# Convolution, attention and expert network on one core: other engines and another order for the last layer norm

## What is computed

```python
logits = jnp.mean(x, axis=1) @ Wr + br                  # softmax twice, top 2 experts of 8
h = gelu(einsum('nd,edf->enf', xf, W1) + b1, approximate=False)
y = einsum('enf,efd->end', h, W2) + b2
out = einsum('ne,end->nd', w_dense, y).reshape(B, S, D)
out = _layer_norm(out + x, gamma, beta)                 # x: the normalised tokens
t = t + out                                             # then back to channels x positions
```

## Time and profile before

| | us |
|---|---|
| median of three runs | 403.71 |
| lowest, highest | 402.61, 403.78 |
| the profiled execution | 403.98 |
| its span (first to last instruction) | 402.2 |
| TensorE, VectorE, ScalarE, GpSimd busy | 385.0, 313.7, 276.1, 152.2 |

### The profile page before, as it was taken

How to read it: one execution, slowest core, us unless ns; L and a number is a source line. 1 busy time by engine, 2 the same in 40 slices (tenths; PEclk the granted TensorE clock), 3 DMA queues, 4 the chain that set the end, 5 groups by cost and what they waited for, 6 DMA issues and landing times.

```text
span 402.2 us, 5828 instructions
## 1 busy us (share of the span) xinstructions
PE 385.0 (96%) x1911; PEld 303.4 (75%) x1916; DVE 313.7 (78%) x699; ACT 276.1 (69%) x530; POOL 152.2 (38%) x205
## 2 busy tenths in 40 slices
PE   8899899999999999999998999999999999997994
PEld 3579896678788888888886888888877777645772
DVE  3798935779989988988998998999898174657745
ACT  1567665568788788888878888888877201557980
POOL 7200005485652754245325278668400000224015
PEclk9999998999999999999999999999999999999999
DMA  7990000000000000000000920000000000000002
GB/s 269 366 346 5 2 2 0 2 1 0 2 1 0 2 0 2 1 0 2 0 0 6 321 99 1 0 2 1 2 0 0 2 0 2 0 0 2 1 0 104
DMA packets 5263, 15.52 MB, mean 39 GB/s; under 512 B 690, under 2 KB 1906, under 8 KB 4978
## 3 DMA queue, kind: packets, MB, share of 16 engines
q1 hardware_dynamic: 4802, 14.19, 9.8%
q10 hardware_dynamic: 432, 0.97, 0.7%
HBM read 14.08 MB, written 1.08 MB: 38 GB/s over the span
## 4 chain that ended last, share of the span: by engine, by line
PE 81%; DVE 9%; ACT 4%; DMA 2%; issue 2%; POOLq 0%; POOL 0%; SPq 0%; ACTq 0%; DVEq 0%
PE ps L1167 13%; PE ps L1169 13%; PE ps L1168 13%; PE ps L1266 7%; DVE nmax_all L1634 3%; PE ps L1149 3%; PE ps L1151 3%; PE ps L1150 3%; PE ps L1050 3%; PE ps L1082 2%; PE ps L1089 2%; PE ps L907 2%; DMA xq<-laid_x_queries 2%; PE ps L1016 2%; PE ps L992 2%
## 5 line engine op out<-in xcount | busy, mean ns | idle before, releaser
L1634 DVE TENSOR_REDUCE nmax_all<-ps 128x1 f32<-128x1024 f32 x128 | 156.2, 1221 | 18.8 <-PE ps L1169 18.1
L780 ACT ACTIVATE exps<-ps,nmax_all 128x1024 bf16<-128x1024 f32 x128 | 142.6, 1114 | 35.1 <-DVE diag_all L1639 34.0
L1167 PE MATMUL ps<-qT_hi,kT_hi 128*128 128x512 f32 x256 | 103.0, 402 | 0.4 <-ACT exps L780 0.4
L1169 PE MATMUL ps<-qT_hi,kT_lo 128*128 128x512 f32 x256 | 100.8, 394 | 0.0
L1168 PE MATMUL ps<-qT_lo,kT_hi 128*128 128x512 f32 x256 | 100.4, 392 | 0.0
L1169 PEld LDWEIGHTS ps<-qT_hi,kT_lo 128*128 128x128 f32 x256 | 48.0, 188 | 10.9
L1167 PEld LDWEIGHTS ps<-qT_hi,kT_hi 128*128 128x128 f32 x256 | 48.1, 188 | 10.6 <-ACT exps L780 3.0
L1168 PEld LDWEIGHTS ps<-qT_lo,kT_hi 128*128 128x128 f32 x256 | 48.1, 188 | 7.4 <-issue 0.2
L525 POOL CAST qT_hi<-xq 128x341 fp32r<-128x341 f32 (+1 forms) x45 | 21.1, 468 | 85.6 <-ACT xq L762 84.3
L527 POOL TENSOR_TENSOR qT_lo<-xq,qT_hi 128x341 fp32r<-128x341 f32 (+1 forms) x45 | 41.6, 925 | 3.6
L1639 DVE CUSTOM_DVE_ANT_0 diag_junk<-ps,ident 128x128 f32<-128x128 f32 x128 | 35.8, 280 | 0.0
(11 more groups left out here) (230 smaller groups left out, 662.1 us busy)
## 6 DMA issues: line engine op xcount, KB each, us to landing
xs_first<-a_store SPq DMA_DIRECT2D x4, 512.0 KB, 5.7
xs_second<-a_store SPq DMA_DIRECT2D x4, 512.0 KB, 9.3
wqkv<-laid_qkv_weights SPq DMA_DIRECT2D x1, 1536.0 KB, 6.7
wvT<-laid_qkv_weights_T SPq DMA_DIRECT2D x1, 1536.0 KB, 10.0
xq<-laid_x_queries SPq DMA_DIRECT2D x2, 512.0 KB, 6.4
xk<-laid_x_keys SPq DMA_DIRECT2D x2, 512.0 KB, 7.9
x<-in_x SPq DMA_DIRECT2D x1, 1024.0 KB, 12.9
w<-in_L_ffn_W SPq DMA_DIRECT2D x1, 1024.0 KB
```

The source lines that it names most:

```text
L780: a.activation(exps[:, n % 2, :], slot(score_slot(col)), ACT.Exp, bias=nmax_all[:, col:col + 1], accum_out=sum_all[:, col:col + 1]).then_i ...
L1167: mm(tgt, keys_hi, qT_hi[:, u % 2, at], start=True, stop=False)
L1169: last = mm(tgt, keys_lo, qT_hi[:, u % 2, at], start=False, stop=True)
L1634: v.tensor_reduce(nmax_all[:, col:col + 1], slot(place), AX_X, ALU.max, negate=True)\
```

## The change

The changed kernel does the same arithmetic. It differs in the last 30 us:

- The rounding of gelu(7), the last step (`LAST_HIDDEN`): ScalarE leaves it out. VectorE rounds half 0 and GpSimd half 1, each with a semaphore of its own, `h_last`, in the place of `h_sb`.
- ScalarE takes the squares of chunks 0 and 1 after gelu(3) and gelu(5), not after gelu(4) and gelu(6), and loads the root's table right behind gelu(7); the square of chunk 2 comes after the root of part 0.
- TensorE takes the variances of chunk 1 one place earlier, and the spread of chunk 0 between the variances of chunks 2 and 3. Two groups of filler, seven matmuls, go.
- VectorE normalises chunk 0 before the reciprocal of chunk 3, and also adds `x1` for chunk 2; GpSimd adds it for chunks 0 and 1 only.

```diff
--- before.py
+++ after.py
@@ -293,12 +293,14 @@
         mb_ready, lg_ps, r_in, r_exp = (sem(n) for n in ("mb_ready", "logits_ps", "r_in", "r_exp"))
         idx_ready, w1_ready, w2_ready = sem("idx_ready"), sem("w1_ready"), sem("w2_ready")
         h_ps, h_full, h_sb, h_lo, y_ps = (sem(n) for n in ("h_ps", "h_full", "h_sb", "h_lo", "y_ps"))
+        h_last = [sem(f"h_last{f}") for f in range(2)]
         b2_centred, w2_mean_ready, w2_centred = (sem(n) for n in (
             "b2_centred", "w2_mean_ready", "w2_centred"))
         xn_hi_ready, xn_lo_ready = sem("xn_hi_ready"), sem("xn_lo_ready")
         late_square = sem("late_square")
         last_diagonal = sem("last_diagonal")
         out_ready = [sem(f"out_ready{c}") for c in range(4)]
+        LAST_HIDDEN = 7
 
 
         LN_PARTS = [((0, 1), (2, 3)), ((0, 1), (2, 3)), ((0, 1), (2,), (3,))]
@@ -602,11 +604,16 @@
                     g.tensor_tensor(w1_lo[:, b, k, :], chosen, w1_hi[:, b, k, :].bitcast(F32), ALU.subtract)\
                         .then_inc(w1_ready, 1)
 
+            n, f = LAST_HIDDEN, 1
+            pool.wait_ge(h_full, 2 * n + f + 1)
+            pool.wait_ge(y_ps, n - 1)
+            g.tensor_copy(hid_hi[:, n % 2, f, :], hid[:, n % 2, f, :]).then_inc(h_last[f], 1)
+
             for c in range(3):
                 pool.wait_ge(LN[2]["rstd"], 1 if c < 2 else 2)
                 lay_diagonal(2, c)
 
-            for c in range(3):
+            for c in range(2):
                 pool.wait_ge(LN[2]["out"], c + 1)
                 at = slice(c * 512, (c + 1) * 512)
                 g.tensor_tensor(conv_o[:, at], centred[:, at], x1[:, at], ALU.add).then_inc(out_ready[c], 1)
@@ -879,6 +886,8 @@
                         act.wait_ge(h_lo, 2 * n - 3 + f)
                     a.activation(hid[:, n % 2, f, :], bank(2 * (n % 2) + f), ACT.Gelu,
                                  bias=b1s[:, b, k, f:f + 1]).then_inc(h_full, 1)
+                    if n == LAST_HIDDEN:
+                        continue
                     act.wait_ge(h_full, 2 * n + f + 1)
                     if n >= 2:
 
@@ -887,11 +896,11 @@
 
             for n in range(8):
                 gelu(n)
-                if n in (4, 6):
-                    square(2, n // 2 - 2)
-            square(2, 2)
+                if n in (3, 5):
+                    square(2, n // 2 - 1)
             load_table(ACT.Sqrt)
             root(2, 0, 6)
+            square(2, 2)
             square(2, 3)
             root(2, 1, 7)
             root(2, 2, 0)
@@ -1353,7 +1362,10 @@
                 if k == 0 and c >= 2:
                     pe.wait_ge(LN[2]["centred"], c - 1)
                 for f in range(FC):
-                    pe.wait_ge(h_sb, 2 * n + f + 1)
+                    if n < LAST_HIDDEN:
+                        pe.wait_ge(h_sb, 2 * n + f + 1)
+                    else:
+                        pe.wait_ge(h_last[f], 1)
                     pe.wait_ge(h_lo, 2 * n + f + 1)
                     tgt = bank(4 + c % 2)
                     mm(tgt, w2_hi[:, b, k, f, :], hid_hi[:, n % 2, f, :], start=(k == 0 and f == 0), stop=False)
@@ -1370,13 +1382,13 @@
                 outputs(n)
                 if n + 2 < 8:
                     hidden(n + 2)
-                if n in (4, 6):
-                    variances(2, 0, 6, n // 2 - 2)
+                if n in (4, 5):
+                    variances(2, 0, 6, n - 4)
             variances(2, 1, 7, 2)
-            keep_warm(3, 4)
+            pe.wait_ge(LN[2]["diagonal"], 1)
+            spread(2, 0, 1)
             variances(2, 2, 0, 3)
-            keep_warm(3, 3)
-            for c in range(3):
+            for c in (1, 2):
                 pe.wait_ge(LN[2]["diagonal"], c + 1)
                 spread(2, c, 1 + c)
             pe.wait_ge(last_diagonal, 1)
@@ -1817,7 +1829,14 @@
             def hidden_remainder(n):
 
                 for f in range(FC):
-                    dve.wait_ge(h_sb, 2 * n + f + 1)
+                    if n < LAST_HIDDEN:
+                        dve.wait_ge(h_sb, 2 * n + f + 1)
+                    else:
+                        if f == 0:
+                            dve.wait_ge(h_full, 2 * n + 1)
+                            dve.wait_ge(y_ps, n - 1)
+                            v.tensor_copy(hid_hi[:, n % 2, f, :], hid[:, n % 2, f, :]).then_inc(h_last[f], 1)
+                        dve.wait_ge(h_last[f], 1)
                     if n >= 2:
 
                         dve.wait_ge(y_ps, n - 1)
@@ -1842,15 +1861,15 @@
                 if c < 3:
                     hidden_remainder(2 * c + 3)
             reciprocals(2, 1)
+            normalise_last(0, 1)
             reciprocals(2, 2)
             lay_diagonal(2, 3, last_diagonal)
-            normalise_last(0, 1)
-            normalise_last(1, 2)
-            normalise_last(2, 3)
-            normalise_last(3, 4)
-            dve.wait_ge(LN[2]["out"], 4)
-            at = slice(3 * 512, 4 * 512)
-            v.tensor_tensor(conv_o[:, at], centred[:, at], x1[:, at], ALU.add).then_inc(out_ready[3], 1)
+            for c in range(1, 4):
+                normalise_last(c, 1 + c)
+            for c in (2, 3):
+                dve.wait_ge(LN[2]["out"], c + 1)
+                at = slice(c * 512, (c + 1) * 512)
+                v.tensor_tensor(conv_o[:, at], centred[:, at], x1[:, at], ALU.add).then_inc(out_ready[c], 1)
 
 
 _INS = ["x", "L0_conv_wq", "L0_conv_bq", "L0_conv_wk", "L0_conv_bk", "L0_conv_wv", "L0_conv_bv",
```

## The result

The changed kernel takes 401.96 us (median of 20 runs, 400.79 to 404.14) where the kernel before takes 403.73 (20 runs, 402.61 to 405.99). The ratio is 0.9955, with a 95% interval of 0.9941 to 0.9969: faster by 0.45%. The forecast was 401.9. The profiled execution took 401.93 us with a span of 400.2, 2.0 less than before.

What follows compares the result with a forecast made beforehand. In the last 30 us, a chain from the last expert product through residual, spreads and last addition bounds the kernel. 0.58+2.21-0.89=1.90, less 0.05, net 1.85 us from 403.98 gives 402.1, median forecast 401.9 us; range 400.8 to 403.2.

Steps and rivals of the forecast that it cites:

- The residual's 0.58: Last residual on VectorE starts 0.09 after its products, 389.93 for 390.51, so chunk 3's square comes 0.58 us earlier.
- The roundings: Last step's roundings leave ScalarE: VectorE's taken as 0.50 us, GpSimd's 0.61, finishing after VectorE's subtraction, at about 387.97.
- (c) of the prediction: Before, VectorE's last addition takes 1.73 us, a same-size subtraction 0.69; it ended 0.56 after GpSimd's third addition.
- The early spread: Chunk 0's spread on TensorE between the last two variances, free at 391.35 when chunk 3's are wanted: nothing to spare.
- The collision: VectorE's diagonal 3, due 0.25 us after GpSimd's first addition begins, waits it out: ends 394.58 instead of 393.69, 0.89 lost.
- Rival 1: VectorE's diagonal 3 gets by GpSimd without waiting and ends at 393.69: 2.6 us less, 401.1 us; chance 0.10.
- Rival 2: GpSimd's rounding costs 1.27 us and waits, half 1's subtraction ends at 389.42, gain shrinks by 0.65: 402.5 us; chance 0.13.
- Rival 3: TensorE's clock falls near the end without fillers: 405.4 us, chance 0.04 for slower; only spread 3 slow, 402.7, 0.05.
- The tail: Last stores after the last addition: issued as before, 0.05 us added for queueing since three come 0.6 us apart.
- The sum: Over the last 30 us: 0.58+2.21-0.89=1.90, less 0.05, net 1.85 us; profiled 403.98 becomes 402.1, median 401.9; chance 0.62.

Runs made afterwards that it cites:

- the front part alone: Changed kernel with the end as before (fillers, block of four spreads, three additions on GpSimd): stretch gelu(7) to last addition 13.51 us, ratio to before 0.9988.
- The fillers' return: Changed kernel with the seven filler products back behind the variances of chunks 2 and 3: stretch 12.88 us for 12.15, ratio to before 0.9966.
- the runs with the overlap gone: Changed kernel with GpSimd's first addition held until diagonal 3 is laid (stretch 11.85 us, ratio 0.9937), or chunk 0's addition on VectorE (11.76 us, 0.9950).
- late squares: Changed kernel with squares of chunks 0 and 1 and variances of chunk 1 at their old places: stretch 12.16 us, one run.
- both on VectorE: Changed kernel with both last roundings on VectorE and GpSimd's removed: stretch 12.16 us, one run.
- the end part alone: Kernel before with fillers gone, early spread of chunk 0 and two additions on VectorE; ScalarE, roundings, squares as before: stretch 13.17 us, ratio 0.9984.
- the eight runs that were repeated: In order: front only, end only, addition held back, roundings on ScalarE, fillers back, neither hand-over nor early spread, before without fillers, addition 0 on VectorE; ratios 0.9937 to 0.9996.
- the run without fillers: Kernel before without its last seven filler products, nothing else: stretch 13.60 us for 14.10, ratio to before 0.9996.

## Why the prediction was right

Each step in us after the start of gelu(7), which was at 385.57 in the profile of before and at 385.39 in that of after:

| step | before | predicted | after |
|---|---|---|---|
| root of part 0 starts | 4.54 | 2.81 | 2.75 |
| half 1's remainder ends | 3.31 | 3.12 | 3.07 |
| outputs(7) end | 4.38 | 4.27 | 4.28 |
| last residual starts | 4.94 | 4.36 | 4.31 |
| chunk 3's square starts (T) | 5.68 | 5.10 | 5.10 |
| diagonal 3 starts | 8.01 | 7.43 | 7.43 |
| diagonal 3 takes | 0.69 | 1.58 | 1.54 |
| last normalisation ends | 12.34 | 11.01 | 10.95 |
| last addition ends | 14.10 | 12.20 | 12.15 |

- **The residual's 0.58.** Right: T came 0.58 earlier, and the front part alone gave 0.59 at the end.
- **The roundings.** VectorE's took 0.43 where I had 0.50, the unshown size. The Trainium skill, "VectorE: DVE Perf Modes", section "Side-by-side: where the cycles go for N=2048 bf16", has a copy between SBUF tiles at two elements a cycle and about 158 cycles of fixed cost, an estimate of (256+158)/0.96=431 ns for 512 columns; its column is for bf16, and for this rounding from fp32 the trace agrees, at 427 ns. GpSimd's took 0.95. No run has it with VectorE idle beside it, so that it stood behind the subtraction, as (c) of the prediction had it, is argued: from its end 0.48 after the subtraction's, and from a rounding of 384 columns in the kernel before, which took 0.50 (L535 at 91.61). That the hand-over to GpSimd gains nothing over VectorE alone I had not seen.
- **The early spread.** Its place fitted with nothing to spare, as written: TensorE was there at 390.34, the diagonal at 389.75, and the variances of chunk 3 began at 391.25 for 391.17 wanted. The fillers' return showed how tight it is. What I did not say is that the two parts need each other; 0.43 of the 1.95 is that. How the 2.22 us from diagonal 3 to the end (5.40 before, 397.54-394.36=3.18 after) divide between the spreads and the moved addition is not shown: no run moves the addition of chunk 2 alone.
- **The collision.** Right in cause and size, 0.85 for 0.89, and in the order of the two, 0.26 us apart for 0.25. Rival 1 is out by the 1.54 itself, and the runs with the overlap gone show that it isn't the diagonal's own: there it takes 0.69. The 0.7 us that rival 1 put on its absence can't be had by moving the overlap, though: that run gained 0.30, since GpSimd's additions, now later, got in the way of VectorE's.
- **Rival 2** (a late rounding) did not come: half 1's remainder ended at 3.07, where rival 2 had 3.85 (389.42-385.57).
- **Rival 3** (the clock) did not come: between 385 and 396 us the granted clock was 1.00 in all twelve profiles, with all seven fillers gone too.
- **The tail.** From the last addition to the span's end I had 0.05 more and it was 0.13 more (400.2-397.54=2.66 for 2.53). The profile gives the span to 0.1 us, so of this 0.13 little more than the sign can be read. The eight kernels whose last three stores become ready 0.54 to 0.61 us apart have 2.61 to 2.71; the kernel before and the front part alone, with two such stores, have 2.53 and 2.61, and the fillers' return, whose last three lie 0.75 and 0.61 apart, has 2.52. That fits some queueing and doesn't prove its size; only the 3.1 with two stores issued together stands clear.
- **The sum.** The stretch gave 1.95 for 1.90, the tail took 0.13, and gelu(7) came 0.18 earlier, for a reason outside the change (gelu(0) was already as much ahead). So the spans are 2.00 apart and the profiled executions 2.05, for a forecast of 1.85. The medians are 1.77 apart: the profiled execution of before lay 0.25 over its median, for which the forecast had taken off 0.27, and that of after 0.03 under. That 401.9 was hit to 0.1 us is still part luck: both medians fell in the same of the two groups of the last section, which lie 1.2 us apart.

## What to carry to other kernels

Where two engines exclude each other, draw both on one time axis before moving work from one to the other. The sum of their work says little: an added wait took 0.30 us off the last stretch, and giving the slower engine a share of a short step made that step 0.13 longer. Follow the chain from its last instruction back, and test parts together as well as apart; here each alone looked like a third or a half of what both gave. And the end of the last computation isn't the end of the kernel: look at which store is issued last and what is in front of it.

## What the runs showed of the hardware

**A VectorE instruction with two SBUF operands and a GpSimd one exclude each other, and the first one wins, even by a tenth of a microsecond.** The diagonal of 512 columns took 0.69 us alone, 1.54 and 1.55 when GpSimd's addition had started 0.26 us earlier, 1.29 when it had started 0.52 earlier. In each of these, and in each addition of VectorE's that was held up, VectorE's ended 0.54 to 0.56 us after GpSimd's: less than its own 0.69. How close the race is, GpSimd's third addition shows, first in the kernel before, then in the same without fillers:

```profile
397.86 1.26 POOL L612 TENSOR_TENSOR conv_e<-xq,x 128x512 f32<-128x512 f32 x1
```

```profile
397.69 1.71 POOL L612 TENSOR_TENSOR conv_e<-xq,x 128x512 f32<-128x512 f32 x1
```

VectorE's last addition began at 397.94 in the first and at 397.57 in the second. With GpSimd 0.08 us ahead, VectorE's took 1.73; with VectorE 0.12 ahead its own took 0.71, and GpSimd's 0.45 more than before. Normalisations with one operand in PSUM took their 0.75 beside GpSimd's additions. I had expected this from the rows of before, but not that it would hold to 0.02 us in every run.

**Some executions lose 1.2 us at one place far from the change, by TensorE's clock.** Most runs of a kernel fall in one of two groups, at 400.8 and 402.0 us for the changed kernel. Two profiles of different groups show where. First the changed kernel, the stretch 60 to 66 us (granted clock is the third number from the end, after the busy times) and the sixteen products in it, then the same of the run with the front part only, whose code is the same up to 380 us:

```profile
60.00:66.00 6.00, 6.00 (x27) 3.80 (x27) 3.29 (x8) 4.11 (x9) 3.11 (x3) 0.72 0.00 0
...
59.76 2.64 PE L1001 MATMUL ps<-w,wvT 128*128 128x128 f32 x16 [0.65 <-ACT fold L712]
```

```profile
60.00:66.00 6.00, 5.40 (x28) 2.91 (x26) 4.56 (x11) 4.55 (x10) 3.12 (x3) 1.00 0.00 0
...
59.66 2.05 PE L1001 MATMUL ps<-w,wvT 128*128 128x128 f32 x16 [0.65 <-ACT fold L712]
```

At 0.72 on average, that is some of the time at 1.2 GHz, the sixteen products take 2.64 us; at 1.00 they take 2.05. The fillers behind them are slow as well. Both come after the same 0.65 us of idle TensorE and the same small products. The second is 0.10 us ahead at their start and 1.31 by the start of gelu(7) (384.08 to 385.39). Three of the profiled executions (front only, late squares, both on VectorE) had 1.00 there and the other nine had 0.72 to 0.77. What decides it in a given execution the runs don't show.

A few executions take 1.6 to 2.1 us more again (403.6 and 404.1 for the changed kernel). The profiled one of the end part alone, 404.64 us, is such a one, and it lost 1.5 of them in the same way elsewhere. First the kernel before, then the end part alone, at 15 us:

```profile
15.19 1.05 PE L948 MATMUL ps<-conv_ws,xk 128*128 128x128 f32 x8
```

```profile
15.00:20.00 5.00, 5.00 (x25) 4.42 (x25) 2.64 (x6) 1.94 (x5) 0.80 (x3) 0.71 0.99 416
...
15.67 1.91 PE L948 MATMUL ps<-conv_ws,xk 128*128 128x128 f32 x8
```

The same eight products take 1.91 us where the mean clock of these 5 us is 0.71, for 1.05 in the kernel before, where it is 1.00, and gelu(7) starts 1.51 later (387.08 for 385.57).

The first of these places alone is worth three quarters of what the change gave, so single runs of this kernel can't be compared with one another. Inside one group they can. In the group of the changed kernel's 402.0 the median is 403.8 for the kernel before, and in the order of the table 403.3, 402.9, 401.5, 402.5, 402.6, 402.3, 403.8 and 401.5 for the eight runs that were repeated. Except for the run without fillers, whose gain went behind the last addition, these differences from before are those of the stretches to 0.15 us.
